# Attention and FP4 feed-forward on one core: a different order of the first projections and gathers, and feed-forward jobs at fixed distances of 15 units

## What is computed

```python
xn = _layernorm(x, axis=-1)
q, k, v = (split_heads(xn @ W + b) for W, b in ((Wq, bq), (Wk, bk), (Wv, bv)))     # 16 heads of 8 columns
scores = einsum('bhqd,bhkd->bhqk', q, k) * 8 ** -0.5 + slope[h] * (pos_k - pos_q)
attn_out = (softmax(scores) @ v) @ Wo + bo
ffn_out = fp4_linear(silu(fp4_linear(xn, w_gate)) * fp4_linear(xn, w_up), w_down)
out = x + attn_out + ffn_out
```

## Time and profile before

| | before |
|---|---|
| median of 3 runs | 824.98 us |
| the profiled execution, its own time | 827.07 us |
| its span in the profile | 825.2 us |
| TensorE matmul (PE) busy | 90% |
| VectorE (DVE) busy | 89% |
| ScalarE (ACT) busy | 81% |
| GpSimd (POOL) busy | 50% |
| granted clock of TensorE, mean | 0.967 |

### The profile page before, as it was taken

How to read it: one execution, slowest core, us unless ns; L and a number is a source line. 1 busy time by engine, 2 the same in 40 slices (tenths; PEclk the granted TensorE clock), 3 DMA queues, 4 the chain that set the end, 5 groups by cost and what they waited for, 6 DMA issues and landing times.

```text
span 825.2 us, 14500 instructions
## 1 busy us (share of the span) xinstructions
PE 742.4 (90%) x4939; PEld 221.1 (27%) x4939; DVE 733.4 (89%) x1338; ACT 665.6 (81%) x1372; POOL 415.0 (50%) x411
## 2 busy tenths in 40 slices
PE   3198999989899999989899999989899999898987
PEld 2011232222232333223132333222232332222223
DVE  8698999999989989899999999999999899999931
ACT  4203988888788988888898989888888889898996
POOL 6447245473536646483545564671634561362551
PEclk9655999999999999999999999999999999999999
DMA  5730001023102002050100102140100100000000
GB/s 149 230 80 2 2 2 54 26 77 78 40 2 41 15 2 77 14 152 5 40 2 4 38 2 91 53 116 2 40 2 2 40 27 2 2 2 2 2 2 26
DMA packets 32848, 31.87 MB, mean 39 GB/s; under 512 B 4360, under 2 KB 26568, under 8 KB 32776
## 3 DMA queue, kind: packets, MB, share of 16 engines
q1 hardware_dynamic: 32776, 30.96, 13.5%
HBM read 15.91 MB, written 15.04 MB: 38 GB/s over the span
## 4 chain that ended last, share of the span: by engine, by line
PE 60%; DVE 26%; ACT 4%; POOL 3%; issue 3%; DMA 2%; SPq 1%; POOLq 0%; ACTq 0%; DVEq 0%
PE mx L1105 22%; PE pv L1133 22%; DVE neg_half L966 20%; PE low L1171 3%; ACT probs L755 3%; PE low L1156 3%; PE low L1150 2%; PE low L1182 2%; PE low L1163 2%; DVE am L935 1%; PE low L1092 1%; DVE ctx_s L987 1%; DVE mb L955 1%; PE low L1144 1%; PE low L1197 1%
## 5 line engine op out<-in xcount | busy, mean ns | idle before, releaser
L966 DVE TENSOR_REDUCE neg_half<-mx 128x1 f32<-128x512 f32 x1024 | 643.8, 681 | 50.5 <-PE mx L1105 43.9
L755 ACT ACTIVATE probs<-low 128x512 f32<-128x512 f32 x1005 | 551.8, 614 | 78.4 <-PE low L1122 67.1
L1105 PE MATMUL mx<-k_op,q_op 51*128 51x512 bf16 x1024 | 335.9, 395 | 58.3 <-DVE neg_half L966 36.7
L1122 PE MATMUL low<-q_op,k_op 53*128 53x512 bf16 x1005 | 316.2, 385 | 0.8 <-DMA q_op<-m_rows 0.8
L1133 PE MATMUL pv<-probs,v_op 128*32 128x512 f32 x2048 | 273.6, 606 | 3.1 <-ACT pv_s L855 1.4
L1105 PEld LDWEIGHTS mx<-k_op,q_op 51*128 51x128 bf16 x1024 | 71.9, 94 | 365.0 <-DVE neg_half L966 298.6
L657 POOL CAST neg_parts<-neg_max 128x16 bf16<-128x16 f32 x31 | 6.8, 220 | 156.0 <-DVE neg_max L972 66.9
L564 POOL TENSOR_SCALAR mb<-mb 128x960 f32<-128x960 f32 (+2 forms) x17 | 58.7, 3456 | 27.2 <-DVE mb L955 25.8
L1122 PEld LDWEIGHTS low<-q_op,k_op 53*128 53x128 bf16 x1005 | 69.0, 93 | 7.6 <-ACT probs L755 5.3
L1133 PEld LDWEIGHTS pv<-probs,v_op 128*32 128x32 f32 x2048 | 40.3, 108 | 88.8 <-ACT probs L755 37.8
L553 POOL TENSOR_TENSOR zb<-hid,inv 128x704 f32<-128x704 f32 x16 | 22.2, 1386 | 54.5 <-DVE inv L950 53.8
(11 more groups left out here) (143 smaller groups left out, 627.6 us busy)
## 6 DMA issues: line engine op xcount, KB each, us to landing
q_op<-q_rows SPq DMA_DIRECT2D x32, 192.0 KB, 3.7
k_op<-k_rows SPq DMA_DIRECT2D x32, 192.0 KB, 4.7
q_rows<-qp SPq DMA_DIRECT2D x8, 384.0 KB, 2.6
k_rows<-kp SPq DMA_DIRECT2D x8, 384.0 KB, 3.0
x_s<-in_L_attn_inputs_dram SPq DMA_DIRECT2D x8, 256.0 KB, 3.6
q_rows<-qp SPq DMA_DIRECT2D x8, 256.0 KB, 2.9
k_rows<-kp SPq DMA_DIRECT2D x8, 256.0 KB, 3.3
out_dram<-o_s SPq DMA_DIRECT2D x7, 256.0 KB, 3.1
```

Source lines behind the costliest of these rows:

```text
L755: nc.scalar.activation(probs[U % 3][:, 2 * g + x, :], bank("exp", U, j), ACT.Exp).then_inc(st_free, 1)
L966: nc.vector.tensor_reduce(neg_half[m % 2][:, i + kh:i + kh + 1], slot("max", pos, kh), AX.X, ALU.max, negate=True).then_inc(mx_free, 1)
L1105: nc.tensor.matmul(slot("max", pos, kh), q, k, start=True, stop=True).then_inc(mx_full, 1)
L1122: nc.tensor.matmul(bank("exp", U, j), k_op[quad][r, g, kt * P:(kt + 1) * P], q_op[quad][r, g, half * HALF:(half + 1) * HALF], start=True, ...
```

## The change

1. Front. The projections of sequence 0 go in the order xnT 0, xnT 1, q 0, k 0, k 1, q 1, v 0, v 1. q and k leave PSUM once (rounded, ScalarE) and VectorE takes the rest straight from PSUM. The scale of q is put into Wq by VectorE. VectorE normalises group 1, ScalarE does the first two steps of the position bias, GpSimd all but one step of the scale of the other 24 tiles. GpSimd clears the operands of quads 0 and 1, makes the third parts one by one, then clears quads 2 and 3. SyncE writes each part when it is there. Quad 0 is gathered in three pieces: what chunks 0 to 7 need (two transfers on SyncE's queue, two on ScalarE's), what chunks 8 to 15 need, and the second half of the queries of heads 0 and 1. VectorE does the statistics of the 24 tiles after the block scales, and `powers(0)` at chunk 2 of the lead. TensorE runs 8 and then 4 matmuls on zeros before the first transposes.
2. Pairs. Pair p starts at unit 6 + 15p, and its jobs lie at 2, 4, 7, 9, 23, 26, 28 and 31 units from there. The projections of later sequences, `ctxT` and `wo` move where units are free. VectorE's steps move to the ends of six different units, GpSimd's `scale_to_grid` to `scale_back` two units later.
3. Maxima. GpSimd's `max_parts(m)` stands in the unit of the turn itself, one unit later in its program. The turn keeps its unit.

```diff
-FFN_FIRST, FFN_LAST = 5, 237
+FFN_FIRST, FFN_STEP = 6, 15
...
-ROUNDED = 10
+FROM_XT = {("gate", 0): 2, ("gate", 1): 4, ("up", 0): 7, ("up", 1): 9, ("hT", 0): 23, ("hT", 1): 26,
+           ("down", 0): 28, ("down", 1): 31}
+ROUNDED = 13
...
-    x_at = put(FFN_FIRST, "xT", 0)
     for p in range(NP):
-        U = put(x_at + 1, "gate", p, 0)
-        U = put(U + 1, "gate", p, 1)
-        U = put(U + 2, "up", p, 0)
-        up = put(U + 1, "up", p, 1)
-        U = put(up + ROUNDED, "hT", p, 0)
-        U = put(U + 1, "hT", p, 1)
-        if p + 1 < NP:
-            x_at = put(FFN_FIRST + (FFN_LAST - FFN_FIRST) * (p + 1) // (NP - 1), "xT", p + 1)
-        U = put(U + 1, "down", p, 0)
-        put(U + 1, "down", p, 1)
+        start = FFN_FIRST + FFN_STEP * p
+        U = put(start, "xT", p)
+        for kind, t in FROM_XT:
+            U = U + (ROUNDED if (kind, t) == ("hT", 0) else 1)
+            if p + 1 < NP or kind in ("gate", "up"):
+                U = max(U, start + FROM_XT[kind, t])
+            U = put(U, kind, p, t)
...
-            U = norm_unit(b) + 1 + 8 * (g % 2)
+            U = norm_unit(b) + 1 + 4 * (g % 2)
...
-        U = put(at["pvT", hb // 2 * 8 + 6 + hb % 2] + 2, "ctxT", hb)
+        U = put(max(U + 1, at["pvT", hb // 2 * 8 + 6 + hb % 2] + 2, at["down", 2 * hb + 1, 1]), "ctxT", hb)
         for i in range(2):
-            U = put(max(U, at["down", 2 * hb + 1, 1]) + 1, "wo", hb, i)
+            U = put(max(U, at["down", 2 * hb + 1, 1]) + 1 + i, "wo", hb, i)
...
+PROJECTIONS = (("xnT", 0), ("xnT", 1), ("q", 0), ("k", 0), ("k", 1), ("q", 1), ("v", 0), ("v", 1))
+FIRST_PARTS = (("q", 0), ("k", 0), ("k", 1), ("q", 1))
...
+            def first_parts_to_dram():
+                sp.wait_ge(st_free, ST["q", 0] + 1)
+                q_part(0, 0)
+                sp.wait_ge(bias_ok, 1)
+                sp.dma_start(bias_rows, bias_p).then_inc(bias_out, 16)
+                sp.wait_ge(two_parts_ok, 1)
+                q_part(0, 1)
+                sp.wait_ge(st_free, ST["k", 0] + 1)
+                k_parts(0, 2)
+                sp.wait_ge(two_parts_ok, 2)
+                k_parts(0, 1)
+                sp.wait_ge(parts_ok, 1)
+                q_part(0, 2)
+                sp.wait_ge(st_free, ST["k", 1] + 1)
+                k_parts(1, 2)
+                sp.wait_ge(two_parts_ok, 3)
+                k_parts(1, 1)
+                sp.wait_ge(parts_ok, 2)
+                k_parts(0, 0)
+                sp.wait_ge(bias_out, 16)
+                sp.wait_ge(ones_ok, 1)
+                bias_rows_in(0)
+                sp.wait_ge(parts_ok, 3)
+                k_parts(1, 0)
+            def last_parts_to_dram():
+                sp.wait_ge(two_parts_ok, 4)
+                q_part(1, 0)
+                q_part(1, 1)
+                sp.wait_ge(parts_ok, 4)
+                q_part(1, 2)
...
+            def first_gather():
+                sp.wait_ge(parts_out[0], PARTS_IN)
+                sp.wait_ge(parts_out[1], PARTS_IN // 2)
+                for x in range(2):
+                    first_rows(sp, k_op, k_rows, x)
+                last_parts_to_dram()
+                sp.wait_ge(parts_out[1], PARTS_IN)
+                for to, rows in ((q_op, q_flat), (k_op, k_flat)):
+                    for x in range(2):
+                        r0 = (2 + x) * HROWS
+                        sp.dma_start(to[0][XROWS * x:XROWS * x + HROWS, 1, :], rows[r0:r0 + HROWS, 0:S]).then_inc(
+                            gathered[0], 16)
+                for x in range(2):
+                    sp.dma_start(q_op[0][XROWS * x:XROWS * x + HROWS, 0, HALF:S],
+                                 q_flat[HROWS * x:HROWS * x + HROWS, HALF:S]).then_inc(half_in, 16)
...
-            sp.wait_ge(bias_ok, 1)
-            sp.dma_start(bias_rows, bias_p).then_inc(bias_out, 16)
-            sp.wait_ge(ones_ok, 1)
-            sp.wait_ge(bias_out, 16)
-            for quad in range(QUADS):
+            first_parts_to_dram()
+            first_gather()
+            for quad in range(1, QUADS):
+                sp.wait_ge(ones_ok, quad + 1)
                 bias_rows_in(quad)
-            for g in range(2):
-                parts_to_dram(g)
-            for quad in range(QUADS):
                 gather(0, quad)
...
+            clear_operands(0)
+            clear_operands(1)
+            for n, (name, g) in enumerate(FIRST_PARTS):
+                last_part(n, name, g)
+            clear_operands(2)
+            clear_operands(3)
...
+            norm_scale_rest()
...
-                    if U == turn_unit(m) - 1:
+                    if U == turn_unit(m):
                         max_parts(m)
...
-                    if U == up + 3:
+                    if U == up + 5:
                         scale_to_grid(p + 1)
-                    if U == up + 5:
+                    if U == up + 7:
                         add_power(p + 1)
-                    if U == up + 7:
+                    if U == up + 9:
                         take_power(p + 1)
-                    if U == up + 8:
+                    if U == up + 10:
                         scale_back(p + 1)
...
+            act.wait_ge(ln_ok, 1)
+            normalize()
             act.wait_ge(bqs_ok, 1)
-            act.wait_ge(ln_ok, 1)
-            normalize(0)
-            keep_xnT(0)
-            normalize(1)
-            keep_q(0)
-            keep_k(0)
-            keep_v(0)
-            keep_xnT(1)
-            keep_q(1)
-            keep_k(1)
-            keep_v(1)
+            for name, g in PROJECTIONS:
+                {"xnT": keep_xnT, "q": keep_q, "k": keep_k, "v": keep_v}[name](g)
+            act.wait_ge(ones_ok, 1)
+            act.wait_ge(parts_out[0], PARTS_IN)
+            for x in range(2):
+                first_rows(act, q_op, q_rows, x)
             std(1)
...
+            def two_parts(n, name, g):
+                j = "qk".index(name)
+                dve.wait_ge(st_free, ST[name, g] + 1)
+                nc.vector.scalar_tensor_tensor(qk_r[g][j], bank(name, g), (bqs_s if name == "q" else bk_s)[:, 0:1],
+                                               qk_p[g][j][:, 0, :], ALU.add, ALU.subtract).then_inc(r_ok, 1)
+                dve.wait_ge(r_ok, n + 1)
+                nc.vector.tensor_copy(qk_p[g][j][:, 1, :], qk_r[g][j]).then_inc(two_parts_ok, 1)
...
+            nc.vector.memset(warm[:], 0.0).then_inc(warm_ok, 1)
             mark(nc.vector.memset(v_op[0][:], 0.0))
             norm_stats(0)
-            norm_scale(0)
-            settle()
+            norm_scale()
+            dve.wait_ge(qkv_in, QKV_IN)
+            nc.vector.tensor_scalar(wq_s[:], wq_s[:], SCALE, None, ALU.mult).then_inc(wq_ok, 1)
+            normalize()
             nc.vector.memset(v_op[0][:, :, :, D:D + 1], 1.0).then_inc(v_zero_ok, 1)
             alibi()
+            dve.wait_ge(bqs_ok, 1)
+            for n, (name, g) in enumerate(FIRST_PARTS):
+                two_parts(n, name, g)
             dve.wait_ge(ident_ok, 1)
             nc.vector.tensor_copy(ident_b[:], ident[:]).then_inc(ident_b_ok, 1)
-            for g in range(2):
-                two_parts(g)
-            norm_stats(1)
-            norm_scale(1)
             weight_maxima()
             x_maxima(0)
             block_scales(0)
             block_inverses(0)
+            norm_stats(1)
+            dve.wait_ge(std_ok, 2)
+            nc.vector.reciprocal(ln[:, 2, LN_TILES[1]], ln[:, 1, LN_TILES[1]]).then_inc(rest_ok, 1)
             for pos in range(LEAD):
-                if pos == 8:
+                if pos == 2:
                     powers(0)
                 reduce_chunk(pos)
...
                         if (U, i) == (up0 + 1, 1):
                             x_maxima(p + 1)
-                        if (U, i) == (up0 + 2, 0):
+                        if (U, i) == (up0 + 2, 1):
                             hidden_maxima(p + 1, 0)
-                        if (U, i) == (up1 + 2, 0):
+                        if (U, i) == (up1 + 2, 1):
                             hidden_maxima(p + 1, 1)
-                        if (U, i) == (up1 + 2, 1):
+                        if (U, i) == (up1 + 3, 1):
                             block_scales(p + 1)
-                        if (U, i) == (up1 + 3, 0):
+                        if (U, i) == (up1 + 4, 1):
                             block_inverses(p + 1)
-                        if (U, i) == (up1 + 4, 1):
+                        if (U, i) == (up1 + 6, 1):
                             powers(p + 1)
...
+                if pos == 0 and kh == 0:
+                    pe.wait_ge(bias_in[0], BIAS_IN)
+                    pe.wait_ge(first_in, GATHERED)
+                elif pos == 8 and kh == 0:
+                    pe.wait_ge(gathered[0], GATHERED)
+                elif pos == 16 and kh == 0:
+                    pe.wait_ge(half_in, GATHERED // 2)
...
+            keep_busy(8)
             pe.wait_ge(ident_ok, 1)
-            project("xnT", 0)
-            pe.wait_ge(qkv_in, QKV_IN)
-            project("q", 0)
```

(62 more changed lines are left out.)

105 lines of the change are left out of this document (54 added, 51 removed).

## The result

| | before, its runs | after |
|---|---|---|
| median | 825.09 us (824.71 to 826.59, 6 runs) | 811.38 us (810.39 to 812.44, 6 runs) |
| ratio | | 0.983, interval 0.9816 to 0.9844 |
| profiled execution, span | 827.07, 825.2 us | 812.44, 810.6 us |

The change takes 13.7 us off; 22.3 were forecast, and 811.38 lies inside the range. The page of the kernel after: its span, the busy times of the engines, and the granted clock in tenths over 40 slices.

A forecast was written before the change was run, and what follows sets the result against it. No engine has much to spare, so who is late for whom was taken to bound the kernel. Terms -7.9 - 2.4 - 10 - 3.5 + 1.5 = -22.3 us took the median of 824.98 to 802.7 us; range 789 to 814.

The forecast's parts named there:

- Front: Up to the first reduction: it starts at 32.9 against 40.80, with VectorE late next; -7.9 us, bounds -10 and -4.8.
- Lead: Before the first score matmul: GpSimd's long steps end before VectorE splits the first maxima; -2.4 us, bounds 0 and -3.2.
- At most 1: In the lead: VectorE's cast of 3.39 us, held by a GpSimd instruction, becomes at most 1 us.
- Pairs: Units 3 to 246: spread VectorE steps save 10 us (bounds 2 and 17), fewer waits for hT 3.5 (0 to 5).
- The two steps that were forecast: In the units: stall per pair falls from 1.5 to about 0.8 us, -10 us; hT waits shrink, -3.5 us.
- Maxima: At turns m=7 and 22: the split behind GpSimd's add_power comes late, about 0.75 us each; +1.5 us (0 to +5).
- End: Attention of the last half, then Wo: it keeps its chain, so 0, within 1 us.
- A: Rival: only the front gains, since VectorE's sum of work bounds the units; 814.7 us, down to 811; chance 0.2.
- B: Rival: everything fits, unit stalls fall to a few us and VectorE meets no lock in the front; 785 us; chance 0.15.
- C: Rival: slower, as GpSimd's split of the maxima comes late for most of 31 turns; 846 us; chance 0.04.
- D: Rival: no front gain, as a piece of quad 0 is late; first reduction at 38 or later, 808 to 811; chance 0.08.
- The signs to look for: Expected profile: units 3 to 246 in about 699 us, single 0.3 us stalls between a pair's steps, turns waiting at m=7 and 22 only.

The follow-up runs named there:

- e3_maxima_back: The changed kernel with GpSimd's split of the maxima back one unit earlier in its program; 807.23 us, ratio 0.9771.
- e10_maxima_two: The changed kernel with the split of the maxima back in its old unit for m=7 and m=22 only; 805.49 us, ratio 0.9752.
- e7: The changed kernel with four matmuls of constants ahead of TensorE's wait for the last row maxima; 811.49 us, ratio 0.9829.
- e2_pairs_only: The kernel before with the new planner and new steps, but the old front and old place of the maxima's split; 814.39 us, ratio 0.9862.
- e5_no_warm: e3_maxima_back without the 12 matmuls on zeros ahead of the first transposes; 805.24 us, ratio 0.9756.
- e8_ctx_first: e3_maxima_back with GpSimd waiting, at the head of its unit behind each pvT, for VectorE's context product; 803.6 us, ratio 0.9737.
- e12_best_b: e8_ctx_first without the 12 matmuls on zeros, and the maxima's split one unit later for all turns but m=7 and m=22; 804.24 us, ratio 0.9736.
- e1: The kernel before with the new front only; pairs, steps and place of the maxima's split stay old; 819.24 us, ratio 0.9919.

## Why the prediction was right, and where not

- **Front, -8.1 against -7.9.** The first reduction is at 32.66 against 32.9 forecast, within its bounds. VectorE is late next, not the transfers, as said: TensorE's first maximum matmul starts at about 28.5 and the reduction waits 4 us more for VectorE. The wait of the three casts beside GpSimd was counted at 0.5 us each; they took 0.83 us each where the first, with GpSimd not on a third part yet, took 0.43. Part of the agreement is luck: Wq and the normalising were counted at 1.0 us and took 2.4 (10.16 to 12.52), and the bias cast was counted at 1.4 and took 0.68, so the bias ended at 16.0 where 15.5 was forecast; what follows the last cast took 11.0 us where 11.5 was counted.
- **Lead, -3.3 against -2.4.** "At most 1" for the cast was too careful, it is 0.17 us. GpSimd had its two 3.62 us steps behind it at 49.2. The clock was 0.50 throughout, and nothing came of warming.
- **Pairs, -11.2 against -13.5** (e3_maxima_back's units against before's). The two steps that were forecast came: over the eight units from `up` 1 on the stalls fall from 24.7 to 12.6 us in after, 12 us where 10 was forecast (the prediction's 22.4 counts five units), and no hT matmul waits for GpSimd. What the step left out is that shifted steps of GpSimd land on other things. First, the context products: they met 2.2 us instructions of GpSimd at units 84, 100, 204 and 220, with 4.7 us of stalls. Before had such meetings at units 28 and 52 (products of 1.24 and 1.33 us, stalls of 1.10 and 1.12), 2.2 us in all; its stall of 1.05 at unit 84 was the hT job of the earlier trace rows. Second, the 1.9 us at units 22 and 142, where `scale_to_grid` stood behind the old place of the split. The product of 1.33 us in before:

```profile
224.30 1.33 DVE L987 TENSOR_TENSOR ctx_s<-pv_s,pv_r 128x128 f32<-128x128 f32 x1
```

- **Maxima, +4.7 against +1.5.** Right in the place, m=7 and 22 and no other turn, and in the mechanism. The term was mis-sized: 0.75 us a turn was counted, for the maxima's way to unit 8m, and 1.87 a turn was measured, all of it at the turn itself: the split came 3.3 us after the maxima were there (214.36 to 217.62), and units 56 and 176 then didn't wait. 3.7 less what units 22 and 142 win (1.5, by e10_maxima_two) leaves 2.2 us, and about 2.6 more stand at units 100 and 101, behind a fall of the clock that e3, e7 and e10 did not have. e7 has the moved split and no such fall, so the move alone doesn't bring it; whether it has a part in it is open. e10_maxima_two confirms the two turns.
- **End, +4.1 against "0, within 1 us".** This is the step that failed. "Keeps its chain" was true of the instructions and not of the transfers: 24 more instructions in TensorE's stream, the warming matmuls counted at nothing, moved its instruction load onto the last write of the maxima. The write lands 1.8 us later than in before (3.1 against 1.4 us after its issue), and the clock fall behind the idle time is about 1.6 us more, by e7_tail_fill; half a microsecond comes with the pairs (e2_pairs_only). Without the warming matmuls unit 248 starts 1.8 us sooner and the end is 1.4 us shorter (e5_no_warm against e3_maxima_back, which has no fall there).
- **Rivals.** A falls by e2_pairs_only, B since some 25 us of stalls are left in the units, C since two turns wait and not 31, D since TensorE's wait for the gathered keys was over by 28.5. The signs to look for named single stalls of 0.3 us; the stalls behind the split and the context products are 0.9 to 3.7.
- The median lies 8.7 us above the forecast. In the profiles 7.7 of it are 4.1 from the end and 5.4 from the units, less 1.8 that front, lead and first units gave beyond their terms; the last 1 us is that the profiled execution stood 2.1 us above its median before and 1.1 above it after.

## What to carry to other kernels

Before moving an instruction to another unit, look at what the *other* engines' long instructions then stand beside, on both sides: a small VectorE product costs 0.3 or 1.6 us by that alone, and one wait on the engine that has slack can cost less than the long product does (e8_ctx_first: 3.7 us gained). When a helper step moves behind a long one of the same engine, move it only in those turns where nothing long is queued ahead, and look again once another wait is put in (e12_best_b). And an edit at the front can change the end: anything that alters the number of instructions shifts the instruction loads, so compare kernels whose counts differ by stretches, not by their totals alone.

## What the runs showed of the hardware

- An instruction load of TensorE (16 KB, 0.9 to 1.6 us) comes about every 18.5 us from 61 us on (median), 40 in after. A small transfer one of whose packets stands behind it lands 1 to 2 us late: 2.4 to 3.4 us instead of 1.3 to 1.4.
- After idle stretches of 1.28 and 1.98 us in a stream that was otherwise busy TensorE's granted clock fell from 2.4 to 1.2 GHz for 6.8 us (3.4 us in e7, 10.2 at the end of e1); which stall had a fall after it differed between executions (unit 100 in after, not in e3, e7 or e10).
- VectorE's product of two operands that both lie in SBUF, 0.29 us alone, took 1.59 us beside a GpSimd product of two operands. The Trainium skill, SBUF — State Buffer, section "Who interferes with whom", says that such an instruction contends with a GpSimd instruction that reads SBUF. The trace agrees, with 1.59 against 0.29 us; the prediction weighed that section for the casts and not for this product.
